# PixArt-style expert block on one core: zero products from the constant tile, two anchor products with the conditional columns stationary

## What is computed

```python
nx = layer_norm(x, ln_gamma, ln_beta)
q, k, v = nx @ Wq, prototype_bank @ Wk, prototype_bank @ Wv
weights = softmax(einsum('bth,bph->btp', q, k) * H ** (-0.5))
evidence = einsum('btp,bph->bth', weights, v)
anchor = broadcast_to(global_anchor[:, None, :], nx.shape)      # cond, one row per batch
combined = concatenate([nx, evidence, anchor], axis=-1)
router_probs = softmax(combined @ router_W + router_b)
h = silu(einsum('btc,ecr->bter', combined, e_w1) + e_b1)
routed = sum((einsum('bter,erh->bteh', h, e_w2) + e_b2) * router_probs[..., None], axis=-2)
g = sigmoid(silu(combined @ gate_w1 + gate_b1) @ gate_w2 + gate_b2)
return x + g * (routed @ out_w + out_b)
```

## Time and profile before

| | |
|---|---|
| median of 3 runs | 429.4 us (429.02 to 430.08) |
| the profiled execution's own time | 428.63 us |
| its span, first to last instruction | 426.8 us |
| PE busy | 421.0 us (99%) |
| DVE busy | 337.7 us (79%) |
| ACT busy | 248.1 us (58%) |
| POOL busy | 111.7 us (26%) |

### The profile page before, as it was taken

The page is one execution under the profiler, slowest core; times in us unless marked ns, Lnnn a source line. Parts: engine busy times, 40 slices in busy tenths (PEclk is TensorE's granted clock), DMA queues, the critical chain, the costliest instruction groups (busy, mean ns, idle before and its releaser), DMA issues.

```text
span 426.8 us, 5938 instructions
## 1 busy us (share of the span) xinstructions
PE 421.0 (99%) x1934; PEld 345.5 (81%) x1934; DVE 337.7 (79%) x702; ACT 248.1 (58%) x381; POOL 111.7 (26%) x105
## 2 busy tenths in 40 slices
PE   8999999999999999999999999999999999999995
PEld 7578888878788888888888888888888888888885
DVE  3878689899899888895788888895788868664376
ACT  3366855868465667474665567474665567465440
POOL 2300362142225032402125032402125022402430
PEclk9999999999999999999999999999999999999998
DMA  8888877327532664443632634443632534132302
GB/s 253 247 208 209 197 187 141 94 68 205 124 95 54 163 150 109 124 111 89 147 99 51 183 78 111 123 115 85 147 100 49 136 76 111 27 69 83 72 0 49
DMA packets 79939, 50.58 MB, mean 119 GB/s; under 512 B 58558, under 2 KB 68326, under 8 KB 79910
## 3 DMA queue, kind: packets, MB, share of 16 engines
q1 hardware_dynamic: 77552, 48.09, 45.1%
q0 software_dynamic: 1152, 1.85, 1.6%
q10 hardware_dynamic: 1206, 0.29, 0.3%
HBM read 27.56 MB, written 7.93 MB: 83 GB/s over the span
## 4 chain that ended last, share of the span: by engine, by line
PE 96%; DVE 2%; DMA 1%; issue 1%; SPq 0%; ACT 0%; DVEq 0%
PE bank L654 40%; PE bank L915 34%; PE bank L900 12%; PE bank L780 2%; PE bank L708 1%; PE bank L750 1%; PE bank L675 1%; DMA work<-in_ctx_dram 1%; PE bank L736 1%; PE bank L683 1%; DVE work L1514 0%; PE bank L695 0%; DVE quad L1516 0%; PE bank L816 0%; DVE xq L1517 0%
## 5 line engine op out<-in xcount | busy, mean ns | idle before, releaser
L654 PE MATMUL bank<-nx,w1n 128*128 128x512 f32 x672 | 171.4, 391 | 0.0
L1141 ACT ACTIVATE hf<-bank,zb 128x512 f32<-128x512 f32 x112 | 77.2, 690 | 121.9 <-PE bank L900 119.5
L654 PEld LDWEIGHTS bank<-nx,w1n 128*128 128x128 f32 x672 | 125.8, 188 | 26.6 <-issue 0.5
L915 PE MATMUL bank<-h,w 128*128 128x512 f32 x552 | 140.2, 389 | 0.0
L915 PEld LDWEIGHTS bank<-h,w 128*128 128x128 f32 x552 | 103.6, 188 | 21.7
L1545 DVE TENSOR_TENSOR h<-hf,h 128x512 fp32r<-128x512 f32 x111 | 85.0, 770 | 35.7 <-ACT h L1145 33.9
L1145 ACT ACTIVATE h<-bank,zb 128x512 fp32r<-128x512 f32 x111 | 75.8, 683 | 0.0
L900 PE MATMUL bank<-wT,vw 128*128 128x512 f32 x224 | 69.7, 392 | 0.0
L900 PEld LDWEIGHTS bank<-wT,vw 128*128 128x128 f32 x224 | 41.9, 188 | 9.3 <-issue 0.5
L1582 POOL TENSOR_TENSOR xq<-xq,quad 128x512 f32<-128x512 f32 x14 | 20.4, 1479 | 110.3 <-DVE quad L1214 110.3
L1597 POOL TENSOR_TENSOR work<-work 128x512 f32<-128x512 f32 x14 | 18.8, 1346 | 68.6 <-DVE work L1462 58.7
(11 more groups left out here) (181 smaller groups left out, 482.6 us busy)
## 6 DMA issues: line engine op xcount, KB each, us to landing
vw<-vw_pair SPq DMA_DIRECT2D x48, 256.0 KB, 3.7
xn<-in_x_dram SPq DMA_DIRECT2D x8, 512.0 KB, 4.0
p_bc<-prob_dram SPq DMA_DIRECT2D x8, 512.0 KB, 5.3
xq<-in_x_dram SPq DMA_DIRECT2D x32, 128.0 KB, 2.5
out_dram<-xq SPq DMA_DIRECT2D x28, 128.0 KB, 2.6
stage<-in_L_xcond_e_w_dram SPq DMA_DIRECT2D x24, 128.0 KB, 4.1
xhat_dram<-xn SPq DMA_DIRECT2D x6, 512.0 KB, 2.8
quad<-xhat_dram SPq DMA_DIRECT2D x24, 128.0 KB, 2.5
```

Of the source, the lines that this page charges most:

```text
L654: mm = pe.matmul(dst, lhs(a), rhs(c), start=first and i == 0, stop=last and i == n - 1)
L915: mm = pe.matmul(bank[place][:, :], lhs, h_tile(s, a), start=c == 0 and i == 0, stop=c == COUNT[g] - 1 and i == 2)
L1141: act.activation(hf[:, s % 2, :], z, ACT.Silu, bias=zb[:, j, b:b + 1]).then_inc(s_h, 1)
```

## The change

`keep_busy` no longer reads a cleared part of `h` but the constant tile of zeros that every program has, as float32, with 128 moving columns in place of 256; the first call has 14 products in place of 12, the wait for DVE's clearing (`s_warm`) and the clearing itself are gone. 

For the gate and the first expert the anchor product is turned round: the conditional columns, padded with zeros to 32 (`cond_cols`), are stationary, and the weights move, 128 columns at a time. Block `c` writes to PSUM partitions 32c to 32c+31. ACT copies the result to SBUF (`z_copy`), PE turns it (`anchor_turn`, "zt" in the plan), and DVE's `z_bias` reads the turned result. The other two experts keep the old form. Around this, `lb_bc`, `exp(0)`, `weights(0)` and `ewt1` move forward in their engines' programs, `pair_lo(0, 1)` and the first expert's `z_bias` back.

```diff
-        warm = h[:, HRING - 1, LO, 0:2 * PART]
+        zeros = nc.const_aps.tensor(0.0, [PART, PART])
...
-        betas = sb("betas", [PART, KC, B])
+        CT, TILED = 32, 2
+        cond_cols = sb("cond_cols", [PART, KC, CT])
+        betas = cond_cols[:, :, B:2 * B]
+        z_rows = sb("z_rows", [PART, PART])
...
-        FIRST_PLAN = {0: ["b2o","ewT0"], 2: ["b2+","rm_+"], 3: ["owhi","fold0","owlo","shi2"], 4: ["px_","ewt1","ehi1", ...
+        FIRST_PLAN = {0: ["b2o","ewT0"], 1: ["zt1"], 2: ["b2+","rm_+"], 3: ["owhi","fold0","owlo","ewt1","shi2"], 4: ["px_","ehi1", ...
...
                 dst = take(ZBIAS_BANK[g], (s_zb, g + 1))
-                for c in range(COUNT[g]):
+                if g < TILED:
                     for k in range(KC):
-                        mm = pe.matmul(dst[:, c * B:(c + 1) * B], stage[:, i, k, c * PART:(c + 1) * PART],
-                                       cols[:, C_COND + k:C_COND + B * KC:KC], start=k == 0, stop=k == KC - 1)
+                        for c in range(COUNT[g]):
+                            mm = pe.matmul(dst[c * CT:(c + 1) * CT, 0:PART], cond_cols[:, k, :],
+                                           stage[:, i, k, c * PART:(c + 1) * PART], start=k == 0, stop=k == KC - 1,
+                                           skip_group_check=True)
...
+            def anchor_turn(g):
+
+                pe.wait_ge(s_zcp, g + 1)
+                n = COUNT[g] * CT
+                pe.transpose(bank[ZBIAS_BANK[g]][:, PART:PART + n], z_rows[0:n, :], ident[0:n, 0:n]).then_inc(s_zbt, 1)
...
                 for _ in range(n):
-                    pe.matmul(bank[7][:, 0:2 * PART], warm[:, 0:PART], warm, start=True, stop=True)
-
-            pe.wait_ge(s_warm, 1)
-            keep_busy(12)
+                    pe.matmul(bank[7][:, 0:PART], zeros, zeros, start=True, stop=True)
+
+            keep_busy(14)
...
             scores(0)
             anchor_product(0)
-            pe.wait_ge(s_pa, PA["vT1"])
-            pair_product(0, 0)
-            pair_product(0, 1)
             pe.wait_ge(s_pv, PV["lb"])
             prep("lb_bc", ...)
+            pe.wait_ge(s_pa, PA["vT1"])
+            pair_product(0, 0)
+            anchor_turn(0)
+            pair_product(0, 1)
...
+            def z_copy(g):
+                n = COUNT[g] * CT
+                act.wait_ge(s_zbc, g + 1)
+                if g >= 1:
+                    act.wait_ge(s_zbt, g)
+                act.copy(z_rows[0:n, :], bank[ZBIAS_BANK[g]][0:n, 0:PART]).then_inc(s_zcp, 1)
...
+            z_copy(0)
             pair_hi(0, 0)
+            exp(0)
             pair_hi(0, 1)
-            exp(0)
...
             w_hi(0)
+            z_copy(1)
...
-            dve.memset(warm.bitcast(F32), 0.0).then_inc(s_warm, 1)
...
+            prep_copy("lb_bc", lb_bc[:, :, :].rearrange("p b c -> p (b c)"), 5, B * RP)
             pair_lo(0, 0)
             z_bias(0)
-            prep_copy("lb_bc", lb_bc[:, :, :].rearrange("p b c -> p (b c)"), 5, B * RP)
+            weights(0)
             pair_lo(0, 1)
-            weights(0)
             w_lo(0)
-            z_bias(1)
```

More of the change, by code:

```diff
@@ L86, in build @@
         SC = NP + 2 * RP
-        VGAP = 32
+        VGAP = 16
         VCOL = VGAP + NCOL
@@ L153, in build @@
         lge = sb("lge", [QROWS, NJ, E])
-        ph = sb("ph", [QROWS, RP * NJ])
-        phT = sb("phT", [QROWS, RP * NJ])
+        ph_pair = sb("ph_pair", [2 * QROWS, RP * NJ])
+        ph, phT = ph_pair[0:QROWS, :], ph_pair[QROWS:2 * QROWS, :]
         ph_et = ph[:, 0:E * NJ].rearrange("p (e j) -> p j e", j=NJ)
@@ L167, in build @@
         WORK = 5120 + 8
-        gap = sb("gap", [PART, 24])
+        gap = sb("gap", [PART, 8])
         raw = ExitStack()
@@ L246, in build @@
         s_gwhi, s_gwlo = sem("s_gwhi"), sem("s_gwlo")
-        s_zbc = sem("s_zbc")
+        s_zbc, s_zcp, s_zbt = sem("s_zbc"), sem("s_zcp"), sem("s_zbt")
         s_zb = sem("s_zb")
@@ L299, in build @@
         PLANS = (FIRST_PLAN, SECOND_PLAN, THIRD_PLAN)
-        PE_STEPS = ("sc", "lg", "vwp", "b2", "fold", "zb")
+        PE_STEPS = ("sc", "lg", "vwp", "b2", "fold", "zb", "zt")
         def plan(engine, b, j, when):
@@ L341, in plan @@
                     "zb": ((n,), {"dve": ["z_bias"]}, {}),
+                    "zt": ((n,), {"dve": ["z_bias"]}, {}),
                     "split": ((n,), {}, {"act": ["w1_hi"], "dve": ["w1_lo"]}),
@@ L747, in anchor_product @@
                 dst = take(ZBIAS_BANK[g], (s_zb, g + 1))
-                for c in range(COUNT[g]):
+                if g < TILED:
                     for k in range(KC):
-                        mm = pe.matmul(dst[:, c * B:(c + 1) * B], stage[:, i, k, c * PART:(c + 1) * PART],
-                                       cols[:, C_COND + k:C_COND + B * KC:KC], start=k == 0, stop=k == KC - 1)
+                        for c in range(COUNT[g]):
+                            mm = pe.matmul(dst[c * CT:(c + 1) * CT, 0:PART], cond_cols[:, k, :],
+                                           stage[:, i, k, c * PART:(c + 1) * PART], start=k == 0, stop=k == KC - 1,
+                                           skip_group_check=True)
+                else:
+                    for c in range(COUNT[g]):
+                        for k in range(KC):
+                            mm = pe.matmul(dst[:, c * B:(c + 1) * B], stage[:, i, k, c * PART:(c + 1) * PART],
+                                           cond_cols[:, k, 0:B], start=k == 0, stop=k == KC - 1)
                 mm.then_inc(s_zbc, 1)
+            def anchor_turn(g):
+                pe.wait_ge(s_zcp, g + 1)
+                n = COUNT[g] * CT
+                pe.transpose(bank[ZBIAS_BANK[g]][:, PART:PART + n], z_rows[0:n, :], ident[0:n, 0:n]).then_inc(s_zbt, 1)
             def b2_product():
@@ L856, in _ @@
             for k in range(KC):
-                pe.matmul(dst[0:B, 0:RP], cols[:, C_COND + k:C_COND + B * KC:KC], wr[:, 2 * KC + k, :], start=k == 0, stop=False)
+                pe.matmul(dst[0:B, 0:RP], cond_cols[:, k, 0:B], wr[:, 2 * KC + k, :], start=k == 0, stop=False)
             for k in range(KC):
@@ L1112, in _ @@
             act.wait_ge(s_pv, PV["cols"])
-            act.copy(betas[:, :, STACK0:], cols[:, C_BETA:C_BETA + KC].unsqueeze(2).broadcast_to([PART, KC, B - STACK0]))\
+            act.copy(betas[:, :, STACK0:], cols[:, C_BETA:C_BETA + KC].unsqueeze(2).broadcast_to([PART, KC, B - STACK0]))
+            act.copy(cond_cols[:, :, 0:B], cols[:, C_COND:C_COND + B * KC].rearrange("p (b k) -> p k b", k=KC))\
                .then_inc(s_betas, 1)
@@ L1357, in z_bias @@
                 blocks = slice(FIRST[g], FIRST[g] + COUNT[g])
-                dve.wait_ge(s_zbc, g + 1)
-                dve.tensor_tensor(zb[:, blocks, :],
-                                  bank[ZBIAS_BANK[g]][:, 0:COUNT[g] * B].rearrange("p (j b) -> p j b", b=B),
+                if g < TILED:
+                    dve.wait_ge(s_zbt, g + 1)
+                    z = bank[ZBIAS_BANK[g]][:, PART:PART + COUNT[g] * CT].rearrange("p (j c) -> p j c", c=CT)[:, :, 0:B]
+                else:
+                    dve.wait_ge(s_zbc, g + 1)
+                    z = bank[ZBIAS_BANK[g]][:, 0:COUNT[g] * B].rearrange("p (j b) -> p j b", b=B)
+                dve.tensor_tensor(zb[:, blocks, :], z,
                                   cols[:, C_B1 + FIRST[g]:C_B1 + FIRST[g] + COUNT[g]].unsqueeze(2)
@@ L1417, in _ @@
             dve.memset(red_nx[:, 0, :], 0.0)
-            dve.memset(betas[:, :, 0:STACK0], 0.0)
+            dve.memset(cond_cols[:, :, B:B + STACK0], 0.0)
+            dve.memset(cond_cols[:, :, 2 * B:], 0.0)
             dve.memset(vr[:, :].bitcast(F32), 0.0)
```

5 lines of the change are left out of this document (2 added, 3 removed).

## The result

The change makes the kernel slower by 0.4%: 430.97 us (430.09 to 432.16, 7 runs) against 429.35 us (428.93 to 430.08, 7 runs), ratio 1.0040 with a 95% interval of 1.0028 to 1.0051. The forecast was 430.6. The profiled execution of the changed kernel took 432.16 us, with a span of 429.1; the one of before took 428.63 with 426.8. That is 3.5 us between two profiled executions and 1.6 between the medians, so the two traces mustn't be subtracted as they stand.

What follows compares the result with a forecast made beforehand. PE, dense after 5.59 us, was taken to bound the kernel. A start loss of 1.45 us (nearer 1.5 from the median) less 0.24 gained at the anchors takes the median from 429.4 to 430.6 us; range 429.3 to 432.0.

Steps and rivals of the forecast that it cites:

- What bounds the kernel: PE, dense after 5.59 us: work added or removed there shows at the end one for one, unless a wait intervenes.
- Zero products leave two records: At PE's start, each float32 zero product leaves two records, so 14 leave 28, from about 0.86 us.
- the first rival: Zero products leave one record each, end before about 4.1 us, and the start loses nothing: 428.6 to 429.2; chance 0.1.
- 1.45, nearer 1.6 in the median: Context turns at PE's start begin 1.45 us late; nearer 1.6 in longer executions, where the clock likely rises later.
- The rival "the clock": PE dense from 0.86 us brings an early clock rise in every run; median 429.8 or 429.9; chance 0.15.
- The landing has slack: The context rows' landing at 5.55 us, which bounded PE's start, now has 1.4 us of slack and absorbs nothing.
- The anchors, 0.24 net: Gate's and first expert's anchor products on PE save 0.78 us, their two added turns cost 0.54: 0.24 saved.
- The failed step: Anchor products overlap only partly, one record's time per product and one more: gate 0.53 us, expert 0.96.
- the second rival: Anchor products in different column quarters overlap fully, about 0.8 us saved net, 430.0 in all; chance 0.2.
- no overlap: Anchor products in different column quarters never run together: 1.1 us lost net, 431.9 in all; chance 0.1.
- The turns, 0.43 and 0.11: Added turns on PE cost 0.43 us at the gate, 0.11 at the first expert; other PE work covers ACT's copies.
- The moved work costs nothing: Work moved on DVE, ACT and SP's queue costs PE nothing; ACT's third block waits from 33.20 until about 34.1 us.

Runs made afterwards that it cites:

- the last two kernels: Six zeros, old layout, second expert's anchors tiled too: 428.28 us; the same with that expert's bias addition moved into DVE's slot 4: 427.73 us.

## Why the prediction was right

The parts measured apart add up to the change only roughly: the start +1.6, the anchors -0.86, the layout +0.5 to 0.6 give 1.3. Measured is 1.6 between the medians, with an interval from 1.2 to 2.2 us, and 1.0 between the median spans. The 0.6 between these two goes with the longer time outside the span in four of seven executions, whose cause is open.

- **What bounds the kernel**: right. PE's lag is 2.25 us near the end of the trace and the profiled span is 2.3 longer, so every loss and gain on PE came out one for one, and no new wait came. The other 1.3 us of the profiled difference is outside the span, of which the prediction says nothing.
- **Zero products leave two records**: right, 28 for 14, from 0.77 (0.86 was forecast). This was the first rival's dividing point, and six products show its other side: there the start costs nothing.
- **1.45, nearer 1.6 in the median**: 1.95 in the kernel that has only this edit, 1.6 without the late DVE step. The size held, but by a clock rise that I took for nearly fixed (3.39 us after the first product) and that the traces show anywhere from 2.8 to 5.9. The profiled execution lost 2.5. The rival "the clock", by which an early dense PE brings an early rise in every run, fell: in the kernel after the rise came 5.9 us after the first product. Its spans scatter over 1.5 us (427.7 to 429.2), its times over 2.1.
- **The landing has slack**: right with fourteen products; with six it bounds the start again.
- **The anchors, 0.24 net**: the term that was mis-sized. I took 0.96 for the expert and 0.53 for the gate; 0.57 and 0.56 were measured, entry not counted. The failed step is "in strict order only the second record of a product can run beside the first of the next". Full overlap was the second rival, with "about 0.8"; by the prediction's own terms it is 0.87 (and no overlap 1.0 lost, not 1.1), and measured is 0.86. The figure that I cited there, from the Trainium skill, TensorE: Matmul & The Clock Gate, Measured speedup vs the span model, gave 0.6 for the expert, and the trace agrees with its 0.57. The gate gains nothing: 0.81 to 0.56 is 0.25, and 0.09 to enter (0.56 us from the second scores' first start to the gate's, 0.47 before) and a turn of 0.20 are 0.29. It has two blocks and so uses two quarters, and takes as long as the expert with four.
- **The turns, 0.43 and 0.11**: 0.20 and 0.11 in the chain, each covered by the work that was named.
- **The moved work costs nothing**: right. ACT's third block began at 35.62, which is the forecast 34.1 and the lag of some 1.6 us.
- **Not foreseen**: 0.5 to 0.6 us for the new places in SBUF. With full overlap the second rival's arithmetic gave 430.0; the layout's cost brought the time back to my forecast. The number was right by luck, two errors of opposite sign and near size: the overlap too small by 0.6, and the layout left out.

## What to carry to other kernels

An edit that declares a tile also moves the tiles behind it: run the old program with the new declarations alone before an edit's gain is believed small. Throw-away products should be counted in records at the lower clock and end before the operand that the first real work waits for lands; one too many is paid in full. Products that use a quarter of the array's columns run four at a time (16 records in 0.57 us here, where 16 of the full width took 1.70), but they bring a copy and a turn, so each hand-over needs a place where the other engines are free (the last two kernels differ by 0.5 us for the place of one 0.18 us addition).

## What the runs showed of the hardware

- The first rise of TensorE's clock came 2.8 to 5.9 us after the first product, and both ends of that range are from kernels with the same fourteen zero products.
- Records of 512 columns are 0.2267 us apart, but mostly 0.229 to 0.236 for about 16 in a row once products read the value weights in the new layout. The experts' columns 64 bytes off alone and the tiles 128 bytes on alone bring 0.29 and 0.23 us of excess, both together 0.62.
- Sixteen records in four column quarters take 0.57 or 0.59 us, by loop order; eight in two quarters take 0.56.
- Two of the nine kernels without DVE's clearing had one DVE step 0.25 to 0.27 us late near 94 us with no cause in the trace; why is open.
- The time beyond the span was 1.8 to 1.9 us in nearly all executions, but 2.7 to 3.2 in four of seven of the kernel after and 2.1 in two of five of the one with its zeros only; why is open.
